# Turning eight columns in the array's transposing mode, at partition 0, instead of multiplying them by the identity at the chunk's partitions

## What is computed

```
x = x + L0(x); x = x + L1(x); x = x + L2(x)        # recurrences over 512 steps
q, k_word, v_word = split(x @ c_attn_w + c_attn_b)
k = concat([cond @ uk_w.T + uk_b, k_word]);  v = concat([cond @ uv_w.T + uv_b, v_word])
scores = where(kj <= qi + 1, q k^T / sqrt(32), -10000) + mask
x = x + (softmax(scores) @ v) @ c_proj_w + c_proj_b
```

## Time and profile before

| | us |
|---|---|
| median of 3 runs | 4057.07 (4054.74 to 4057.52) |
| the profiled execution | 4053.96 |
| span of its trace | 4052.3 |
| TensorE matmul busy in it | 3869.1 (95%) |
| VectorE busy | 2335.6 (58%) |
| ScalarE busy | 1066.0 (26%) |
| mean granted TensorE clock | 0.987 of full |

### The profile page before, as it was taken

The page is one execution under the profiler, slowest core; times in us unless marked ns, Lnnn a source line. Parts: engine busy times, 40 slices in busy tenths (PEclk is TensorE's granted clock), DMA queues, the critical chain, the costliest instruction groups (busy, mean ns, idle before and its releaser), DMA issues. The chain is left out here.

```text
span 4052.3 us, 172362 instructions
## 1 busy us (share of the span) xinstructions
PE 3869.1 (95%) x78452; PEld 2600.6 (64%) x78452; DVE 2335.6 (58%) x8378; ACT 1066.0 (26%) x3931; POOL 159.7 (4%) x374
## 2 busy tenths in 40 slices
PE   6799999999999999999999999999769999999998
PEld 4577776777666699976666666775434555555555
DVE  3565665666566566656555665665325656665664
ACT  1121111111111111111111111111004555555555
POOL 0000000000000000000000000000000000000000
PEclk9999999999999999999999999999979999999999
DMA  5000000000000000000000000001000000000000
GB/s 188 3 4 4 3 3 3 3 3 3 4 3 3 3 4 3 3 4 3 3 4 3 3 3 3 3 3 65 2 6 1 12 9 12 14 12 12 14 7 19
DMA packets 34261, 46.85 MB, mean 12 GB/s; under 512 B 5819, under 2 KB 22251, under 8 KB 33526
## 3 DMA queue, kind: packets, MB, share of 16 engines
q1 hardware_dynamic: 31222, 29.43, 2.3%
q10 hardware_dynamic: 2304, 6.29, 0.4%
HBM read 27.33 MB, written 8.39 MB: 9 GB/s over the span
## 5 line engine op out<-in xcount | busy, mean ns | idle before, releaser
L181 PE MATMUL bank<-wh,h 128*8 128x256 f32 x16384 | 990.1, 381 | 62.1 <-DVE h L356 31.3
L201 PE MATMUL bank<-wh,h 128*16 128x256 f32 (+1 forms) x17408 | 997.1, 369 | 52.4 <-ACT h L237 50.7
L201 PEld LDWEIGHTS bank<-wh,h 128*16 128x16 f32 (+1 forms) x17408 | 529.3, 97 | 338.9 <-ACT h L237 73.5
L181 PEld LDWEIGHTS bank<-wh,h 128*8 128x8 f32 x16384 | 469.1, 90 | 390.7 <-DVE h L356 50.2
L328 DVE STREAM_TRANSPOSE tp<-bank 128x256 f32<-128x256 f32 x512 | 230.5, 450 | 643.0 <-PE bank L181 643.0
L187 PE MATMUL bank<-wh,h 128*8 128x128 f32 x16384 | 549.7, 274 | 0.0
L187 PEld LDWEIGHTS bank<-wh,h 128*8 128x8 f32 x16384 | 444.0, 90 | 117.7 <-issue 2.6
L250 ACT ACTIVATE gates_sb<-pre_sb 128x32 f32<-128x32 f32 x512 | 117.8, 230 | 1356.5 <-DVE pre_sb L330 1356.5
L225 PE MATMUL bank<-stage,w_qkv 128*32 128x128 f32 x11904 | 385.7, 273 | 0.0
L225 PEld LDWEIGHTS bank<-stage,w_qkv 128*32 128x32 f32 x11904 | 342.9, 110 | 44.1
L237 ACT ACTIVATE h<-sum 128x64 f32<-128x64 f32 (+1 forms) x544 | 138.1, 254 | 783.9 <-DVE sum L272 783.9
(11 more groups left out here) (132 smaller groups left out, 3326.6 us busy)
## 6 DMA issues: line engine op xcount, KB each, us to landing
xrows<-in_x_dram SPq DMA_DIRECT2D x32, 256.0 KB, 3.7
out_dram<-X SPq DMA_DIRECT2D x32, 256.0 KB, 2.6
w_qkv<-in_L_cond_c_attn_w_dram SPq DMA_DIRECT2D x1, 3072.0 KB, 18.1
wh<-in_L_cond_w_W_dram ACTq DMA_DIRECT2D x4, 512.0 KB, 8.8
w_qkv<-in_L_cond_w_W_dram ACTq DMA_DIRECT2D x4, 512.0 KB, 10.6
wx<-in_L_cond_Wx_dram SPq DMA_DIRECT2D x2, 1024.0 KB, 8.5
wh<-in_L_cond_Wh_dram SPq DMA_DIRECT2D x2, 1024.0 KB, 10.7
mask_all<-in_mask_Bx1x1xS_ff_dram SPq DMA_DIRECT2D x8, 256.0 KB, 3.2
```

Of the source, the lines that this page charges most:

```text
L181: mm = pe.matmul(mem.ps0[32 * j:32 * j + B, 0:2 * P], h0[:, us, k, ts, :], columns_of(mem.wh0[:, k, 0:3:2, :], j), start=(k == 0), stop=(k ...
L201: mm = pe.matmul(mem.ps12[32 * j:32 * j + B * len(ls), P * l0:P * l1], h12[:, us, k, ts, l0:l1, :].rearrange("p l b -> p (l b)"), columns_ ...
```

## The change

The eight columns of `extras` are turned by the array's transposing mode, as `shares` is, instead of by a product with the identity. Its output then stands at partitions 0 to 7 of the bank, whatever the chunk is, and ScalarE's copy reads it there and writes it to the chunk's partitions.

```diff
                         pe.transpose(bank[:, P:2 * P], mem.shares[:, v % RING, :], mem.ident[:, :])
-                        mm = pe.matmul(bank[FAR * qc:FAR * qc + EXTRAS * HPG, 0:P],
-                                       mem.extras[:, v % RING, :], mem.ident[:, :], start=True, stop=True,
-                                       skip_group_check=True)
+                        mm = pe.transpose(bank[0:EXTRAS * HPG, 0:P], mem.extras[:, v % RING, :], mem.ident[:, :])
                         if image_of(v) is not None:
                             mm = image_products(bank, 2 * P, image_of(v))
```

```diff
                         rows = slice(FAR * qc, FAR * qc + EXTRAS * HPG)
-                        nc.scalar.copy(mem.probs_extra[rows, qc, :], bank[rows, 0:P])
+                        nc.scalar.copy(mem.probs_extra[rows, qc, :], bank[0:EXTRAS * HPG, 0:P])
```

## The result

| | us |
|---|---|
| kernel before, median of 6 runs | 4057.3 (4054.74 to 4064.72) |
| changed kernel, median of 6 runs | 4024.43 (4017.23 to 4029.33) |
| ratio | 0.9916, 95% interval 0.9903 to 0.9930 |
| profiled execution of the changed kernel | 4027.31, span 4025.6 |

The gain is 33 us between the medians, 28 to 39 by the interval. Forecast were 25.7 us and a time of 4031, with a range of 4023 to 4046.

The account below looks back on a forecast made before the run. TensorE's order of work was taken to bound the attention; 29.7 us saved less waits of 1.8 and 2.2 gives 25.7, so 4057.07 becomes 4031 us. Own range 4026 to 4037, stated 4023 to 4046.

Parts of the forecast that it names:

- TensorE's order of work sets the attention's end: Attention, 3068 to 4042 us: TensorE busy 861 of 872 us, so work taken out shortens the time unless a wait appears.
- The second record: L791: one record instead of two for each of 128 units, 0.113 us each, 14.5 us saved.
- The change of division in front: L790 to L791: 0.20 becomes 0.11, or 0.26 becomes 0.16 after a wait; 0.095 less either way.
- The change behind, where L768 or L730 follows: Behind L791, in 38 units: 0.20 becomes 0.11 since both followers are full-width, 0.09 us less each.
- The run behind, L768's or L730's: From L790 to L768 or a second product: 0.52 before, 0.22 after, 0.295 less; 38 units, 11.2 us.
- The wait behind chunk 2: Next unit's fifth L785 waits 0.055 us for ScalarE's copy L882, once in four units: 32 times, 1.8 us lost.
- Waits for the exponentials: First sequence and tail: gains of units just before are waited away, eight waits at 0.27, 2.2 us lost.
- Half time: Rival: the eight-column turning occupies the array half as long, 5 us more saved, 4026; chance 0.12.
- a strip of its own: Rival: the eight-column turning keeps both 0.20 seams, only a record goes, 14.5 less about 1.5 of waits, 4044; chance 0.14.
- The clock: Rival: the clock falls behind each lean stretch, some 28 more falls of 1.5 us, 42 us added, 4073; chance 0.04.

Follow-up runs that it names:

- e4: Changed kernel, with the remaining turning pieces of chunk 1 and 2 units issued ahead of the weighing product instead of behind it; 4016.0 us, ratio to before 0.9905.
- e8: e4 with chunk 3's two remaining pieces of blocks also ahead of the weighing product, shares and the eight columns behind it; 4005.86 us, ratio to before 0.9871.
- e2: Kernel before, with L791 a full-width plain product of all 128 columns of shares with the identity, eight columns left out; 4035.58 us, ratio 0.9952.
- e3: Changed kernel with the turning of the eight columns issued twice in a row; 4034.65 us, ratio to before 0.9953.
- e1: Changed kernel with the eight columns multiplied by the identity again, output at partitions 0 to 7 for every chunk; 4054.73 us, ratio to before 0.9998.
- e5: Kernel before, with the image scores (L768) moved between the turning of shares and the plain eight-column product; one run, 4051.15 us.
- e7: Changed kernel with one more small ScalarE copy ahead of the one that signals, in units of chunk 2 alone; one run, 4018.41 us.
- e6: Kernel before, with L791 a turning of all 128 columns of shares instead of the product of the eight columns; 4022.95 us, ratio 0.9906.

## Why the prediction was right, and where its sizes were off

- **TensorE's order of work sets the attention's end.** Right: what was taken from it arrived in the time, three times over (changed kernel, e4, e8), less what few waits took.
- **The second record.** 14.5 us forecast. e2 has it and the changed kernel hasn't: 0.9952 - 0.9916 = 0.0036, 15 us, with intervals of 7 us to each side; unit by unit e2's steps are 0.11 us longer than the changed kernel's, but for those with waits, as the sum had it. e3 puts a turning of the same size back, 0.11 in each unit.
- **The change of division in front.** 0.095 forecast, 0.20 to 0.11 and 0.26 to 0.16 measured, 128 x 0.095 = 12.2 us. e2 shows that a plain product of full width doesn't have it, e1 that it doesn't hang on the partition.
- **The change behind, where L768 or L730 follows.** 0.20 to 0.11 measured, 38 x 0.09 = 3.4 us, as forecast.
- **The run behind, L768's or L730's.** This term failed: in the step "0.11 + 0.11 = 0.22 after, 0.295 less" I moved the run forward and left its length alone. It got 0.10 shorter with both (0.95 for 1.05, 3.60 for 3.70): 31 x 0.10 = 3.1 us and 7 x 0.10 = 0.7 us. A hint was there: L785's first record, "whose weights nothing hides", is 0.05 longer, and L768 with 4 moving columns depends on loads altogether. e5 shows it for L768 with nothing else changed but the order.
- **The wait behind chunk 2.** 1.8 us forecast, 0 measured. The lateness of the load was right, 0.05 us, but I let it count in full. A load normally starts 0.11 ahead of its matmul and needs less; the first 0.05 of lateness is free, and what comes on top counts, as e7 shows. The factor of 32 was wrong too, against the prediction's own count: in 7 of these units L730 follows, and the load isn't late there.
- **Waits for the exponentials.** 2.2 us forecast. Between the starts of L790 of successive units, seven steps gained nothing or little (those from units 5, 8, 121, 122, 124, 125 and 126, counted from 0); by the gain that they should have had this is about 1.5 us. The forecast multiplied by 0.27 per wait, a figure that it doesn't derive; its own sum gives 29.7 / 128 = 0.23 per unit.
- **Half time, or a strip of its own.** Both fell: the turning takes 0.11 us (e3), whatever it loads (e6), and stands 0.11 behind L790. By the Trainium skill (TensorEngine Tiling (Array Packing), Restrictions and Key Properties) column tiling excludes the transposing mode for FP32, and a change of tiling mode drains TensorE; the traces agree, 0.11 for 0.20. Of the Trainium skill's "4× faster for FP32" (TensorE: Matmul & The Clock Gate, Terms) the runs show a factor of two: one record of 0.11 us for the plain product's two (e6 and e2, both of 128 columns).
- **The clock.** It was no lower on the whole: 0.99 of full up to 3947 us and 0.97 in the tail (before 0.99 and 0.98). In the attention it stood at the half level for 17 us before and for 15 us in the changed kernel. The fall in the run of L726 and its like at 3681 us did not come again; one at 3546 us was new. Why it falls where it does stays open.

```profile
3075.00:3947.00 872.00, 860.89 (x7038) 491.53 (x7039) 560.16 (x1721) 514.49 (x1684) 37.92 (x236) 0.99 0.04 11
3947.00:4025.60 78.60, 65.68 (x608) 40.86 (x606) 37.21 (x109) 41.54 (x129) 2.94 (x16) 0.97 0.08 21
```

Sum with the measured sizes: 14.5 + 12.2 + 3.4 + 3.1 + 0.7 - 0 - 1.5 = 32.4 us. The medians lost 32.9 (28 to 39), the attention of the two profiled executions 33.6. The difference to the latter is the clock: it fell in units 0, 1, 32, 64 and 80 in one of the two or at another moment, and the steps from these five gained 1.3 us more together than their like. So the mechanism held, and the forecast of 25.7 us was 7 us low by the sizes of its terms: 3.8 for the run behind, 1.8 for the wait behind chunk 2, 0.7 for the exponentials, and what remains is rounding and the clock. All three err the same way. The measured 4024.4 lies below the forecast's own range (4026 to 4037), and inside the stated one (4023 to 4046) only because that reached down to the half-time case, which e3 refutes. That part of the hit is luck.

## What to carry to other kernels

Where TensorE is the bound and its jobs are small, count the changes between full width, column strips and row strips in its order: each cost 0.09 us at the seam here, and 0.05 to 0.10 more in the run that follows, whose first weight load is then not hidden. A narrow product that uses a sixteenth of the array can be dearer than a full-width one; and jobs of one width put side by side, as in e4, save without any less work. A job of 1 us put over a wait for a copy of 0.59 us hides it, as in e8.

## What I had not expected of the hardware

- The first matmul behind a change of array division is longer by its load, 0.05 us for a turning; a run of L768, which streams 4 columns, loses 0.10 us, and so does one of L730, which streams 512.
- A weight load started 0.05 us late, 0.055 us ahead of its matmul instead of 0.11, and the matmul was still on time.
- ScalarE started a copy 0.08 us behind one that is recorded as 0.18 us long: the additional small copy of e7 delayed the next by half of its recorded length.
- Behind the same code, the first L790 stood 3066.5 to 3078.0 us after the start, in ten executions of ten kernels.
